# Attention and feed-forward layer on one core: where row sums, transposed maxima and a causal selection stand, and narrow score tiles packed into PSUM banks

## What is computed

```
qkv = encodings @ W_attn + b_attn                     # q, k, v: (8, 16, 1024, 32)
scores = einsum('bhki,bhqi->bhkq', k, q) / sqrt(32)
scores = where(k_index <= q_index, scores, -10000)    # causal
attn = softmax(scores, axis=2)                        # over the keys
combined = einsum('bhkq,bhkl->bhql', attn, v)
x = layernorm(x + combined @ W_out + b_out)
```

## Time and profile before

| | us |
|---|---|
| median of three timed runs | 2603.3 (2601.86 to 2606.7) |
| the profiled execution | 2603.97 |
| its span | 2602.2 |
| PE, POOL, DVE, ACT busy | 2507.7, 1600.0, 1665.0, 1234.6 |
| attention phase | about the first 1800 us |

### The profile page before, as it was taken

How to read it: one execution, slowest core, us unless ns; L and a number is a source line. 1 busy time by engine, 2 the same in 40 slices (tenths; PEclk the granted TensorE clock), 3 DMA queues, 4 the chain that set the end, 5 groups by cost and what they waited for, 6 DMA issues and landing times.

```text
span 2602.2 us, 40583 instructions
## 1 busy us (share of the span) xinstructions
PE 2507.7 (96%) x13920; PEld 1821.6 (70%) x13920; DVE 1665.0 (64%) x4231; ACT 1234.6 (47%) x2354; POOL 1600.0 (61%) x1666
## 2 busy tenths in 40 slices
PE   7899999999999999999999999998999999999998
PEld 5565666667666667666667666674588888888886
DVE  6666667667767767777676677667465535544533
ACT  2555566566665666665666565665631111111110
POOL 1676788887888787888787888887241213122211
PEclk8998999999999999999999999998999999999999
DMA  7556567676666866657676576764430101011010
GB/s 144 91 97 129 115 151 167 127 152 145 139 143 126 171 141 137 155 130 141 127 181 126 119 175 127 142 130 131 155 106 33 33 25 41 17 30 36 17 33 17
DMA packets 167263, 286.46 MB, mean 110 GB/s; under 512 B 23121, under 2 KB 58001, under 8 KB 165906
## 3 DMA queue, kind: packets, MB, share of 16 engines
q1 hardware_dynamic: 159890, 267.01, 47.6%
q0 software_dynamic: 7168, 16.85, 2.0%
HBM read 116.97 MB, written 65.11 MB: 70 GB/s over the span
## 4 chain that ended last, share of the span: by engine, by line
PE 55%; POOL 34%; ACT 4%; issue 3%; DVE 2%; DMA 1%; SPq 0%; POOLq 0%; ACTq 0%; DVEq 0%
POOL Pa L786 29%; PE PS L1467 13%; PE PS L1446 13%; PE PS L1324 6%; PE PS L1412 5%; PE PS L1396 5%; PE PS L1365 4%; PE PS L1316 4%; PE PS L1330 2%; POOL Pm L763 2%; PE PS L1339 1%; POOL P L763 1%; ACT Pm L909 1%; DMA Kp<-nat 1%; POOL lnrs L799 1%
## 5 line engine op out<-in xcount | busy, mean ns | idle before, releaser
L786 POOL TENSOR_TENSOR Pa<-Pa,Pm 128x512 f32<-128x512 f32 (+1 forms) x623 | 770.9, 1258 | 153.7 <-ACT Pm L909 96.4
L1396 PE MATMUL PS<-Qp,Kp 98*128 98x512 f32 (+3 forms) x1536 | 550.9, 363 | 31.5 <-ACT Pm L909 13.1
L909 ACT ACTIVATE Pm<-PS 128x512 f32<-128x512 f32 (+3 forms) x856 | 395.4, 471 | 294.4 <-PE PS L1396 240.3
L1365 PE MATMUL PS<-Kp,Qp 96*128 96x512 f32 (+3 forms) x1536 | 500.6, 362 | 14.9 <-DMA Kp<-nat 5.1
L1006 DVE TENSOR_REDUCE nm<-PS 128x1 f32<-128x512 f32 x512 | 344.4, 685 | 193.2 <-PE PS L1365 192.5
L1396 PEld LDWEIGHTS PS<-Qp,Kp 98*128 98x128 f32 x1536 | 292.2, 192 | 241.8 <-ACT Pm L909 119.6
L786 POOL TENSOR_TENSOR Pa<-Pa,P 128x512 f32<-128x512 f32 (+1 forms) x307 | 381.8, 1263 | 73.3 <-ACT P L909 46.2
L876 ACT ACTIVATE G<-PS,b1c 128x512 f32<-128x512 f32 x128 | 88.2, 689 | 539.6 <-PE PS L1446 539.6
L1014 DVE CUSTOM_DVE_ANT_0 PS<-PS,maskA,nm 128x384 f32<-128x384 f32 (+3 forms) x512 | 263.3, 554 | 116.0 <-PE PS L1365 112.4
L1014 DVE CUSTOM_DVE_ANT_0 PS<-PS,maskA 128x384 f32<-128x384 f32 (+3 forms) x512 | 245.0, 506 | 137.9 <-PE PS L1365 137.9
L1365 PEld LDWEIGHTS PS<-Kp,Qp 96*128 96x128 f32 x1536 | 284.9, 195 | 68.4 <-DVE nm L1014 9.9
(11 more groups left out here) (142 smaller groups left out, 4261.9 us busy)
## 6 DMA issues: line engine op xcount, KB each, us to landing
Qp<-nat SPq DMA_DIRECT2D x192, 256.0 KB, 6.8
Kp<-nat SPq DMA_DIRECT2D x192, 256.0 KB, 5.7
o_s<-Of SPq DMA_DIRECT2D x64, 256.0 KB, 2.1
Ot<-o_s SPq DMA_DIRECT2D x64, 256.0 KB
xb<-in_x SPq DMA_DIRECT2D x64, 256.0 KB, 3.3
h_s<-hs SPq DMA_DIRECT2D x64, 256.0 KB, 3.4
out<-xb SPq DMA_DIRECT2D x64, 256.0 KB, 3.5
x_raw<-in_xt SPq DMA_DIRECT2D x15, 1024.0 KB, 6.4
```

The source lines that it names most:

```text
L786: e.tensor_tensor(to, to, probs(u, k)[:, h0:h0 + many, 0:w], ALU.add).then_inc(s["padd"], many)
L909: e.activation(probs(u, k)[:, h_, 0:w], PS[:, B_BANKS[j % 2], 0:w], ACT.Exp).then_inc(s["b_exp"], 1)
L1365: ins = e.matmul(to, Qp[0:96, u % 4, h_, qt * P:qt * P + P], Kp[0:96, (2 * i + k0 // 512) % 4, h_, 0:w], start=True, stop=True)
L1396: e.matmul(PS[:, B_BANKS[j % 2], 0:w], Kp[0:98, (2 * i + k // 4) % 4, h_, k % 4 * P:k % 4 * P + P], Qp[0:98, u % 4, h_, 512 - w:512], star ...
```

## The change

- **F and N** move. F is put at positions 15.99 and 31.99 of a pair's beats (`F_AT`), N is asked for beat 15 of its slot in both parities (before: 10 and 14, where the queue of dense jobs let it come at beat 14). With the product of step 0 of the even unit two beats earlier, F, N and products stand next to each other on PE.
- **Products** are grouped by `PRODUCTS` and `PV_LAG`: an even unit's steps 1, 2 and 3 run together (before: 1 alone, then 2 and 3).
- **Narrow tiles of pass B are packed**: 256-wide tiles two heads to a bank, 128-wide ones all four to a bank. PE issues the same matmuls, but ACT takes one exponential over the bank, and one bank hand-over replaces two or four. A pair has 38 tiles instead of 48. The tiles' positions are spread over the same beats by their estimated work, so the 512-wide ones stand a little further apart.
- **The last `keep`** of a unit moves ahead of the first addition of the step before it (`h0 == (0 if k + 2 == ksteps(u) else 2)`).

```diff
--- before.py
+++ after.py
@@ -34,13 +34,16 @@
 BEATS = 16
 A_AT = ((0.0, 8.5), (8.5, 30.0))
 B_AT = ((28.0, 36.5), (36.5, 58.0))
-F_LAG = (1.6, 1.6)
+F_AT = (15.99, 31.99)
 A_BANKS = (0, 1, 2)
 B_BANKS = (3, 4)
 PV_BANK = 5
 D_BANKS = (6, 7)
 
-PRODUCTS = (((0,), (1,), (2, 3)), ((0,), (1, 2), (3, 4), (5, 6, 7)))
+
+
+PRODUCTS = (((0,), (1, 2, 3)), ((0,), (1, 2), (3, 4), (5, 6, 7)))
+PV_LAG = ((1, 2), (2, 2, 3, 3))
 
 UP_BANKS = (0, 1)
 DOWN_BANK = 2
@@ -62,8 +65,14 @@
     return 12 * (u // 2) + 4 * (u % 2)
 
 
-def tiles_before(u):
-    return 4 * ksteps_before(u)
+def tiles_of(u, k):
+
+    w = width(u, k)
+    return [(0, 1, 2, 3)] if w == P else [(0, 1), (2, 3)] if w == 2 * P else [(h_,) for h_ in range(HG)]
+
+
+def tiles_before(u, k=0):
+    return 38 * (u // 2) + 11 * (u % 2) + sum(len(tiles_of(u, x_)) for x_ in range(k))
 
 
 def chunks(u):
@@ -142,7 +151,7 @@
     if job[0] == "N":
         if by_products(job[1]):
             return 13 if job[1] % 2 else 8
-        return 14 if job[1] % 2 else 10
+        return 15
     if job[0] == "O" and job[1] == B - 1:
         return (8, 0, 4, 8, 12, 0, 4, 8)[job[2]]
     if job[0] == "T":
@@ -233,16 +242,17 @@
             for j, x in enumerate(some):
                 p = u // 2 * 2 * BEATS + at + (end - at) * sum(work[:j]) / sum(work)
                 ring.append((p, ("A", u, j, x)))
-            ring.append((u // 2 * 2 * BEATS + end + F_LAG[u % 2], ("F", u)))
+            ring.append((u // 2 * 2 * BEATS + F_AT[u % 2], ("F", u)))
             at, end = B_AT[u % 2]
-            work = [168 + 0.87 * width(u, t // 4) for t in range(4 * ksteps(u))]
-            for t in range(4 * ksteps(u)):
+            some = [(k, hh) for k in range(ksteps(u)) for hh in tiles_of(u, k)]
+            work = [168 + 0.87 * width(u, k) * len(hh) for k, hh in some]
+            for t, (k, hh) in enumerate(some):
                 p = u // 2 * 2 * BEATS + at + (end - at) * sum(work[:t]) / sum(work)
-                self.tiles.setdefault(int(p), []).append((p, (u, t // 4, t % 4)))
-                self.formed[u, t // 4] = int(p)
+                self.tiles.setdefault(int(p), []).append((p, (u, k, hh)))
+                self.formed[u, k] = int(p + (end - at) * work[t] / sum(work) * (1 - 1 / len(hh)))
             for k in range(ksteps(u)):
-                k1 = max([g for g in PRODUCTS[u % 2] if k in g][0])
-                n = self.formed[u, k1] + (2 if diag(u, k1) is None else 3)
+                j, k1 = [(j, max(g)) for j, g in enumerate(PRODUCTS[u % 2]) if k in g][0]
+                n = self.formed[u, k1] + PV_LAG[u % 2][j]
                 assert not by_products(u) or n < self.beat["N", u]
                 self.products.setdefault(n, []).append((u, k))
         self.scored = {}
@@ -278,7 +288,7 @@
 
     def steps_formed(self, n):
 
-        return [x[:2] for x in self.score_tiles(n) if x[2] == 3]
+        return [x[:2] for x in self.score_tiles(n) if x[2][-1] == HG - 1]
 
     def pv_steps(self, n):
 
@@ -474,11 +484,11 @@
 
         def tiles_read(u, k):
 
-            return s["b_mm"], tiles_before(u) + 4 * k
+            return s["b_mm"], tiles_before(u, k)
 
         def formed(u, k):
 
-            return s["b_exp"], tiles_before(u) + 4 * k + 4
+            return s["b_exp"], tiles_before(u, k + 1)
 
         last_x = max(T.x_users[B - 1, c] for c in range(2))
         last_o = T.number["O", B - 1, TT - 1]
@@ -780,7 +790,7 @@
                         w = width(u, k)
                         many = 1 if w > 256 else 2 if w > P else HG
                         for h0 in range(0, HG, many):
-                            if h0 == 2 and kept_early(u, k + 1):
+                            if h0 == (0 if k + 2 == ksteps(u) else 2) and kept_early(u, k + 1):
                                 keep(u, k + 1)
                             to = acc[:, u % 2, h0:h0 + many, 512 - w:512]
                             e.tensor_tensor(to, to, probs(u, k)[:, h0:h0 + many, 0:w],
@@ -889,11 +899,11 @@
             for n in range(T.first, T.last):
                 if n == v_first:
                     split_v(0)
-                for u, k, h_ in T.score_tiles(n):
-                    j = tiles_before(u) + 4 * k + h_
+                for u, k, hh in T.score_tiles(n):
+                    j = tiles_before(u, k) + tiles_of(u, k).index(hh)
                     w = width(u, k)
                     e.wait_ge(s["b_mm"], j + 1)
-                    if h_ == 0:
+                    if hh[0] == 0:
                         a = added(u, k)
                         if k == 0 and u >= 2:
                             e.wait_ge(*done(("N", u - 2)))
@@ -906,7 +916,9 @@
                                 e.wait_ge(*done(("N", u0)))
                             else:
                                 e.wait_ge(s["p_sum"], k0 + 1 + (ksteps(U - 2) - 1) * (u0 % 2))
-                    e.activation(probs(u, k)[:, h_, 0:w], PS[:, B_BANKS[j % 2], 0:w], ACT.Exp).then_inc(s["b_exp"], 1)
+                    e.activation(probs(u, k)[:, hh[0]:hh[-1] + 1, 0:w],
+                                 PS[:, B_BANKS[j % 2], 0:len(hh) * w].rearrange("p (h n) -> p h n", n=w),
+                                 ACT.Exp).then_inc(s["b_exp"], 1)
                 if n in copied:
                     u = copied[n]
                     b, g, c = unit(u)
@@ -1385,16 +1397,19 @@
                 else:
                     a_piece(j, *x_[1:])
 
-            def b_tile(u, k, h_):
+            def b_tile(u, k, hh):
                 i, c = u // 2, u % 2
-                j = tiles_before(u) + 4 * k + h_
+                j = tiles_before(u, k) + tiles_of(u, k).index(hh)
                 w = width(u, k)
-                if k == 0 and h_ == 0:
+                if k == 0 and hh[0] == 0:
                     e.wait_ge(s["shift"], 32 * (u + 1))
                 if j >= 2:
                     e.wait_ge(s["b_exp"], j - 1)
-                e.matmul(PS[:, B_BANKS[j % 2], 0:w], Kp[0:98, (2 * i + k // 4) % 4, h_, k % 4 * P:k % 4 * P + P],
-                         Qp[0:98, u % 4, h_, 512 - w:512], start=True, stop=True).then_inc(s["b_mm"], 1)
+                for x_, h_ in enumerate(hh):
+                    ins = e.matmul(PS[:, B_BANKS[j % 2], x_ * w:x_ * w + w],
+                                   Kp[0:98, (2 * i + k // 4) % 4, h_, k % 4 * P:k % 4 * P + P],
+                                   Qp[0:98, u % 4, h_, 512 - w:512], start=True, stop=True)
+                ins.then_inc(s["b_mm"], 1)
 
             def pv(u, k):
                 b, g, c = unit(u)
```

## The result

The changed kernel takes 2568.45 us (median of four runs, 2566.62 to 2572.62) against 2604.75 for the kernel before beside it (four runs, 2601.86 to 2606.7): ratio 0.9864, interval 0.985 to 0.9879. It is 36 us faster where 21 were forecast (2582), inside the range of 2560 to 2602. The profiled execution took 2572.62 us, 31.3 less than the one before.

The account below looks back on a forecast made before the run. A loop through PE, ACT and POOL bounds each pair: 21.00 + 33.50 + 0.27 = 54.77 us. Gains 0.12 + 0.6 + 0, say 0.75 a pair, over 28.5 pairs give 21 us: 2582, range 2560 to 2602.

Parts of the forecast that it names:

- The loop of sums, PE and ACT, POOL and sums again: Period of a pair of units: 21.00 us to POOL's start, 33.50 of POOL, 0.27 to the next sums.
- The last selection: Moved ahead of one addition: wait shifts from last product to sums; 0.12 us a pair gained, bounds 0 to 0.27.
- no PE idle there: Sign of being right: PE no longer idles at the unit's last product for its selection.
- Regrouping and packing behind the sums: PE work from sums to POOL's start: savings and additions sum to about 0 a pair, bounds −0.5 to +0.4.
- Ln and Exp hidden: Score tiles behind the sums no longer wait for exponentials queued behind Ln and Exp on ACT: 0.6 us a pair.
- POOL's stretch: POOL's unbroken work from its start to the unit's last addition: stays 33.50 us.
- The long pairs: Every fourth pair, 57.51 us instead of 54.77: same loop with slower additions, so the same gain.
- The rule on tiling: Mode changes drain TensorE, 0.26 us a visit; read alone, three visits save 0.9 us a pair, 28 us.
- Case 1: Wait does not return at the sums, PE's savings count in full: 1.9 us a pair, 2549 us; chance 0.08.
- Case 2: Stall behind the sums nearer 1.19, semaphore gives 0.27: 1.3 us a pair, 2566 us; chance 0.15.
- Case 3: Dense matmuls moved behind the sums eat most of the gain: 0 to 0.15 a pair, 2599 to 2603; chance 0.12.
- Case 4: POOL starves at step 2 of the odd unit, 0.7 us spare: slower, 2624 us; chance 0.08.

Follow-up runs that it names:

- K: The kernel before with only the last selection moved ahead of an addition; 2596.34 us, ratio 0.9977.
- G: The kernel before with only F, N and the products regrouped; 2602.36 us, ratio 0.9998.
- P: The kernel before with only the narrow tiles of pass B packed, and the tile spacing that follows; 2625.52 us, ratio 1.0077.
- K+G: The changed kernel with the packing of narrow tiles undone; 2576.05 us, ratio 0.9901.
- K+P: The changed kernel with the regrouping of F, N and products undone; 2617.06 us, ratio 1.0049.

## Why the prediction was right

**What bounds the kernel.** The loop of sums, PE and ACT, POOL and sums again stood up in every experiment. One reading was wrong in its detail: the 0.27 between the last addition and the sums is no latency. In the kernel before, the sums come 0.15 + 2.83 behind the last selection, by PE's own work, and POOL's last addition is done a little earlier. So the path there ran through POOL up to the selection, and then through PE. K alone shows the latency itself, 0.05.

**The last selection.** Forecast 0.12 a pair, bounds 0 to 0.27; measured 0.21, since the latency is the 0.05 just named and not the 0.15 taken from the product. The mechanism (no wait at the product, one at the sums) came as said: 0.4 us of waiting, forecast "up to about 1.0". The product still starts 0.15 behind its selection (941.54 and 941.69 above), so "no PE idle there" was wrong by the letter: the product before it would let it start at about 941.61, which leaves 0.08, and it is outside the loop. The two tiles' waits ahead of the sums, 0.55, cost nothing here, as the prediction said.

**Regrouping and packing behind the sums.** Forecast 0, bounds −0.5 to +0.4. Counted at the paces, PE's work from sums to step 1's last tile is 19.29 before and 19.20 after: −0.09. The parts, too, came near: G by itself takes 0.71 off and P puts 0.62 back, where the prediction's items are −0.88 and +0.84.

**Ln and Exp hidden.** Forecast −0.6; the rest of that distance (waits and the way through ACT) went from 1.73 to 1.11, −0.62. But this is a sum of two: G takes some 0.4 of waiting away and brings a new wait of 0.35 at the first 128-wide tile, which P takes away again. The prediction entered nothing for packing, and it is P that keeps this term whole; that the 0.6, a choice between 0.29 and 1.19, was met so closely is luck. The packed 128-wide tile itself cost what was entered for it, 0.39 − 4 × 0.07 = 0.11 against 0.15.

**POOL's stretch.** Forecast unchanged at 33.50; it is 33.3. Of these 0.2, K has 0.05 (the gap of 0.17 us ahead of step 6's addition at 958.46 is one of 0.12 now) and P, next to G, 0.12 to 0.14 (33.42 to 33.30, 33.48 to 33.34). The traces show where P's part lies, in a collision of POOL with DVE for which the prediction had entered 0. In the kernel before it is the selection that took 1.09 instead of 0.63 beside DVE's subtraction. In K+G the subtraction starts at 932.34 and POOL's next 384-wide addition takes 1.46 us where the others take 1.01. After the change these are the rows, of DVE and of POOL:

```profile
935.71 0.69 DVE L1222 TENSOR_TENSOR Os<-Ot,Os 128x512 fp32r<-128x512 f32 x1
```
```profile
935.94 1.34 POOL L796 TENSOR_TENSOR Pa<-Pa,Pm 128x384 f32<-128x384 f32 x1
```

The subtraction now starts 0.23 ahead of a 384-wide addition and costs it 0.33 instead of 0.45. That the 0.12 between them is all of P's part is a reading of these rows; no run isolates it.

**The sum.** 0.71 + 0.20 + 0.21 = 1.1 us for the ordinary pair, against 0.75. Over the 23 pairs of the table the mean gain is 1.22 (1275.84 to 1247.75 us), 28 us. The long pairs did not gain the same, as forecast, but 1.7 each. The pairs before give 7.5, and behind the sums of unit 61 the change gives 3.7 back (799.1 to 802.7 to the end of the span), which the prediction had not looked at. 28.1 + 7.5 − 0.6 − 3.7 = 31.3, the profiled difference (the −0.6 from the last pair, 62.5 to 63.1). So the mechanism held and three sizes were too small: the latency at the sums, POOL's stretch, and the long pairs. The timed medians differ by 5 us more than the profiled executions, for which nothing here accounts.

**The rule on tiling.** The Trainium skill (TensorEngine Tiling (Array Packing), Key Properties) says that a change of tiling mode drains TensorE. With the prediction's price for the visits the change was worth 28 us through PE. G alone takes three visits a pair away, 1.0 us of PE's work a pair, and gains nothing: in this order what PE loses at a visit while the product waits for POOL anyway costs no time. On K+P, where the sums to POOL's start is the path, G brings 49 us, more than the 31 of its PE work.

**The rivals.** Case 1 (the wait doesn't come back) fell to the 0.33 us idle at the sums. Case 2 had the right neighbourhood (2566) for a wrong reason, an Ln and Exp stall near 1.19. Case 3's mechanism, dense matmuls that move behind the sums, is real, and P alone shows it: +0.79. Case 4 didn't come: POOL has 0.62 us to spare at step 2.

## What to carry to other kernels

With every engine over half busy in the stretch that counts and one at 97%, measure the loop: take one instruction that recurs, and split its period into stretches between engines. An edit is worth what it takes from a stretch on that loop. The same edit can be worth nothing alone and 49 us where the others are in place, as G was, so test each by leaving it out of the set as well as by adding it. When one engine's work is proved to set the loop by making it slower, ask next what makes it start late: a wait on a whole step where one head would do was worth 30 us, nearly as much as the 36 of the three edits together.

## What the runs showed of the hardware

- The 32-column fp32 matmuls of sums and product side by side take 1.86 us (945.53 to 947.39 above). Alone they take 1.00 each, and the row behind each is 0.1 longer.
- POOL's fp32 additions with 128 partitions: 1.27 us for 512 columns, 0.70 for 256 (5.62 / 8), 0.22 for 32 (0.88 / 4). Splitting one costs some 0.14 (5.62 against 5.03 for four).
- The same DVE subtraction of two SBUF tensors made a selection of POOL 0.46 us longer (1.09 against 0.63), or an addition 0.45 (1.46 against 1.01) or 0.33 (1.34), by where in POOL's work it started.
- A matmul that waits for POOL starts 0.05 us behind the addition's end at the sums and 0.15 behind the selection's end at the product. Why they differ stays open.
- Four 128-wide score matmuls in a row take 0.39 us, single ones between wider matmuls 0.07 each.
